# A DCN ranker on one core: ScalarE hands the copies out of PSUM to VectorE and fetches more embedding rows one by one

## The chip, the cores and the metric

One Trainium2 chip, of which the kernel uses one core. The metric is the device time of one launch in microseconds (us), the median of several runs; lower is better. In the traces PE is TensorE (PEld its weight loads), DVE is VectorE, ACT is ScalarE, POOL is GpSimd and SP is SyncE. A letter q behind an engine's name (ACTq, SPq) means its instruction queue: what the sequencer does without keeping the engine's lanes busy, such as issuing a DMA.

## What is computed

The reference, cut to what matters:

```python
def ref(ids, emb, cross_w, cross_b, w1, b1, w2, b2, w3, b3, out_w, out_b):
    x0 = emb[ids].reshape(2048, 26 * 64)      # 26 fields, rows of 64 floats, table of 125000 rows
    x = x0
    for i in range(3):
        s = x @ cross_w[i]
        x = x0 * s[:, None] + cross_b[i] + x
    h = relu(x0 @ w1 + b1)                    # 1664 -> 1024
    h = relu(h @ w2 + b2)                     # 1024 -> 512
    h = relu(h @ w3 + b3)                     # 512 -> 256
    return sigmoid(concatenate([x, h], axis=1) @ out_w + out_b)
```

All of it is float32. Every sample needs 26 rows of 256 bytes out of the embedding table.

## The kernel before

**Tiles.** The 2048 samples are 16 tiles of 128. For every tile the 26 embedding rows of each sample are gathered into `x_buf[t % 2]` (128 partitions by 1664 columns). A chunk is 128 of these columns, two fields; a tile has 13 chunks in four groups of 4, 3, 4 and 2 (`GROUPS`). For a group, VectorE patches rows whose index lies past the table (`make_whole`, L516; it also is the sign that the group is there), TensorE transposes its chunks into a PSUM bank (`transpose_x`, L729), and the transposed block is split into a high and a low part: ScalarE copies it out as `xT_hi` (`x_hi`, L400), VectorE subtracts that from the bank to give `xT_lo` (`x_lo`, L523). Each product of float32 matrices is then three matmuls, hi·hi, hi·lo and lo·hi (`three_passes`, L717). For `w1` a chunk is nine matmuls in three PSUM banks.

**A step.** In step t TensorE does layer 2 of tile t-1 and layer 1 of tile t, with transposes between the chunks; then it transposes `h1` of tile t (L771) and does layer 3 of tile t-1. The hidden layers are split as the inputs are: ScalarE makes `h1T_hi` (L406) and `h2T_hi` (L411) with a Relu, VectorE the low parts (L528). VectorE also adds the biases (L535, L544, L562). Step 0 also loads and splits the weights, and the last step has code of its own.

**Who fetches the rows.** GpSimd gathers one field of a tile with one indirect DMA (L347). Its order is field by field, held back by waits on `chunk_done` (`PACED`, `BEHIND`) and by `other_engines_turn`. A few fields are left out of it (`of_pool`) and are fetched row by row, 128 small DMAs for a field of a tile: SyncE takes field 24 in nine tiles (L295), ScalarE field 25 in seven tiles (L387), 400 fields being left for GpSimd. Both load the byte addresses into registers first (L292, L384) and write into small landing buffers, four of SyncE's and two of ScalarE's. When all 128 rows are there, ScalarE copies them into `x_buf` (`sp_place` L372, `act_place` L394). Group 3, the last of a tile, is the one whose `make_whole` waits for these copies.

**ScalarE's order.** It runs in program order: in a step it issues shares of 8, 12, 4, 16, 12 and 12 rows (64 in all), and between them come its six copies out of PSUM and the placing.

```python
            def step(t):
                fetch(ACT_SHARES[0])
                x_hi(t, 0)
                fetch(ACT_SHARES[1])
                h2_hi(t - 1)
                fetch(ACT_SHARES[2])
                x_hi(t, 1)
                fetch(ACT_SHARES[3])
                x_hi(t, 2)
                ...
```

The functions that the diff touches, with what calls them:

Of the kernel before, what the change touches and what calls it, by code (L numbers as in the profile page):

```python
# [5 lines left out]
def dcn_ranker_kernel(nc, r_ids, emb, cross_w, cross_b, w1, b1, w2, b2, w3, b3, out_w, out_b, out):  # L6
# [29 lines left out]
    def groups(t):  # L36
        return LAST_GROUPS if t == TILES - 1 else GROUPS
# [6 lines left out]
    LOW_BITS = 2 ** (H.bit_length() - 1) - 1  # L44


    SP_TILES = [2, 4, 6, 8, 9, 10, 12, 14, 15]
    SP_REGS = 32
    SP_FIELD = F - 2
    SP_BUFS = 4  # L50
    assert SP_FIELD // FPK in GROUPS[-1] and SP_FIELD // FPK in LAST_GROUPS[3]

    ACT_TILES = [3, 5, 7, 9, 11, 13, 15]
    ACT_FIELD = F - 1
    ACT_BUFS = 2
    ACT_SHARES = [8, 12, 4, 16, 12, 12]
    assert ACT_FIELD // FPK in GROUPS[-1] and all(
        sum(ACT_SHARES) * (t - 1) >= P * (j + 1) for j, t in enumerate(ACT_TILES)) and P % sum(ACT_SHARES) == 0  # L60


    ROW = E * 4
# [43 lines left out]
    with ctx:  # L107
# [44 lines left out]
        act_rows = [ids[:, (SP_BUFS + j) * E:(SP_BUFS + j + 1) * E].bitcast(F32) for j in range(ACT_BUFS)]  # L152
        sp_cols = ids[:, (SP_BUFS + ACT_BUFS) * E:(SP_BUFS + ACT_BUFS) * E + ONE_BY_ONE].bitcast(F32)
        at_bytes = sb("at_bytes", [ONE_BY_ONE, P], I32)
        at_row = {t: i for i, t in enumerate([t for t in SP_TILES if t % 2 == 0] + [t for t in SP_TILES if t % 2])}

        VR = (2 * CROSS + 1) * K1
        vec_rows = sb("vec_rows", [VR, P])
# [117 lines left out]
        @block.sync  # L276
        def _(sync):
            sync.dma_start(ids[:, :], r_ids.rearrange("(p t) f -> p (t f)", p=P)).then_inc(ids_loaded, 16)
            for n, (name, k, m) in enumerate(LOADS):
                src = {"w1": w1, "w2": w2, "w3": w3}[name][k * P:(k + m) * P, :].rearrange("(m p) c -> p m c", m=m)  # L280
                sync.dma_start(parts(n)[0], src).then_inc(weights_loaded[n], 16)

            sync.wait_ge(idx_ready, 3)
            for rows, vec in ((b1_rows, b1), (b2_rows, b2), (b3_rows, b3), (out_w_rows, out_w[D:D + N3, 0]), (out_b_rows, out_b)):
                sync.dma_start(rows[:, :], vec.rearrange("(o n) -> o n", o=1).broadcast_to([P, rows.shape[1]])).then_inc(rows_loaded, 16)
            sync.wait_ge(sp_idx_ready, 1)
            for i, t in enumerate(SP_TILES):
                if i >= SP_BUFS:
                    sync.wait_ge(sp_placed, i - SP_BUFS + 1)
                for p in range(0, P, SP_REGS):  # L290
                    regs = [sync.alloc_register(f"sp_row{i}_{p + j}") for j in range(SP_REGS)]
                    sync.load(regs, at_bytes[at_row[t]:at_row[t] + 1, p:p + SP_REGS])  # L292
                    for j, reg in enumerate(regs):
                        at = sync.snap(reg, donate=True, min_val=0, max_val=(2 * H - 1) * ROW)
                        sync.dma_start(sp_rows[i % SP_BUFS][p + j:p + j + 1, :].bitcast(U8),  # L295
                                       emb_bytes[:, bass.DynSlice(at, ROW)], bounds_check="skip_entire_dma").then_inc(sp_landed[i % SP_BUFS], 16)
            sync.wait_ge(result_ready, 2)
            sync.dma_start(out[:, 0].rearrange("(p t) -> p t", p=P), result[:, :]).then_inc(stored, 16)
            sync.wait_ge(stored, 16)
# [50 lines left out]
        def _(act):  # L350
# [13 lines left out]
            def split_hi(n):  # L364
                raw, hi, _ = parts(n)
                act.wait_ge(weights_loaded[n], 16)
                act.activation(hi, raw, ACT.Copy).then_inc(hi_split, 1)

            def sp_place(t):
                i = SP_TILES.index(t)  # L370
                act.wait_ge(sp_landed[i % SP_BUFS], 16 * P * (i // SP_BUFS + 1))
                act.activation(x_buf[t % 2][:, SP_FIELD * E:(SP_FIELD + 1) * E], sp_rows[i % SP_BUFS],  # L372
                               ACT.Copy).then_inc(sp_placed, 1)
# [2 lines left out]

            def fetch(share):

                j, p = fetched[0] // P, fetched[0] % P
                if p == 0 and j >= ACT_BUFS:  # L380
                    act.wait_ge(act_placed, j - ACT_BUFS + 1)
                row = len(SP_TILES) + j
                regs = [act.alloc_register(f"act_row{j}_{p + i}") for i in range(share)]
                act.load(regs, at_bytes[row:row + 1, p:p + share])  # L384
                for i, reg in enumerate(regs):
                    at = act.snap(reg, donate=True, min_val=0, max_val=(2 * H - 1) * ROW)
                    act.dma_start(act_rows[j % ACT_BUFS][p + i:p + i + 1, :].bitcast(U8),  # L387
                                  emb_bytes[:, bass.DynSlice(at, ROW)], bounds_check="skip_entire_dma").then_inc(act_landed[j % ACT_BUFS], 16)
                fetched[0] += share

            def act_place(t):
                j = ACT_TILES.index(t)
# [33 lines left out]
            def first_step():  # L426
                for g in range(NG):
                    for n in HI_AHEAD[g]:
                        split_hi(n)
                        if n == 0:  # L430
                            cross_hi()
                    x_hi(0, g)
                h1_hi(0)

            def step(t):
                fetch(ACT_SHARES[0])
                x_hi(t, 0)
                fetch(ACT_SHARES[1])
                h2_hi(t - 1)
                fetch(ACT_SHARES[2])  # L440
                x_hi(t, 1)
                fetch(ACT_SHARES[3])
                x_hi(t, 2)
                if t in SP_TILES:
                    sp_place(t)
                if t in ACT_TILES:
                    act_place(t)
                fetch(ACT_SHARES[4])
                x_hi(t, 3)
                fetch(ACT_SHARES[5])  # L450
                h1_hi(t)

            def last_step(t):
                x_hi(t, 0)
                h2_hi(t - 1)
                x_hi(t, 1)
                x_hi(t, 2)
                if t in SP_TILES:
                    sp_place(t)
                if t in ACT_TILES:  # L460
                    act_place(t)
                for g in range(3, len(LAST_GROUPS)):
                    x_hi(t, g)
                h1_hi_last(t)
                h2_hi_last(t)
# [20 lines left out]
        def _(dve):  # L486
# [16 lines left out]
            def make_whole(t, g):  # L503
# [10 lines left out]
                if t in ACT_TILES and ACT_FIELD in range(a, a + n):  # L514
# [2 lines left out]
                                    past[:, t * F + a:t * F + a + n].rearrange("p (f o) -> p f o", o=1).broadcast_to([P, n, E]),  # L517
                                    end_bank.rearrange("p (o e) -> p o e", o=1).broadcast_to([P, n, E])).then_inc(x_whole, 1)

            def x_lo(t, g):  # L520
                dve.wait_ge(xT_hi_ready, NG * t + g + 1)
                ks = groups(t)[g]
                dve.tensor_tensor(xT_lo[:, ks[0]:ks[-1] + 1, :].rearrange("p k b -> p (k b)"), x_bank[g % 2][:, 0:len(ks) * P],  # L523
                                  xT_hi[:, ks[0]:ks[-1] + 1, :].rearrange("p k b -> p (k b)").bitcast(F32),
                                  ALU.subtract).then_inc(xT_ready, 1)
# [40 lines left out]

            def h1_lo(t):
                for half in range(2):
                    dve.wait_ge(h1T_hi_ready, 2 * t + half + 1)
                    part = slice(half * HB, (half + 1) * HB)  # L570
                    relu_lo(h_bank[half], HB * P, h1T_hi[:, part, :].rearrange("p k b -> p (k b)"),
                            h1T_lo[:, part, :].rearrange("p k b -> p (k b)"), h1T_ready)
# [61 lines left out]
                dots_out(0)  # L634
                h1_lo(0)

            def begin(t):
                make_whole(t, 0)
                x_lo(t, 0)
                l2_out(t - 1)  # L640
                h2_lo(t - 1)
                make_whole(t, 1)
                x_lo(t, 1)

            def step(t):
                begin(t)
                for g in range(2, NG):
                    make_whole(t, g)
                    x_lo(t, g)
                l1_out(t)  # L650
                dots_out(t)
                h1_lo(t)
                l3_out(t - 1)

            def last_step(t):
                begin(t)
                l3_out(t - 1)
                for g in range(2, len(LAST_GROUPS)):
                    make_whole(t, g)
# [30 lines left out]
            link(dve.tensor_scalar(past[:, 0:QUICK], ids[:, 0:QUICK], float(H), None, ALU.is_ge))  # L690
            dve.wait_ge(idx_ready, 3)
            copied = 0
            for field, tiles in ((SP_FIELD, [t for t in SP_TILES if t % 2 == 0]), (SP_FIELD, [t for t in SP_TILES if t % 2]),
                                 (ACT_FIELD, ACT_TILES)):
                every = tiles[1] - tiles[0]
                assert tiles == list(range(tiles[0], tiles[-1] + 1, every))
                a, b = (t * F + field for t in (tiles[0], tiles[-1]))
                dve.scalar_tensor_tensor(out=sp_cols[:, copied:copied + len(tiles)], in0=past[:, a:b + 1:every * F], scalar=float(H),
                                         in1=idx[:, a:b + 1:every * F], op0=ALU.mult, op1=ALU.add).then_inc(sp_cols_ready, 1)
                copied += len(tiles)  # L700
# [11 lines left out]
        def _(pe):  # L712
# [195 lines left out]
            pe.transpose(h_bank[0][:, 0:VR], vec_rows[:, :], identity[0:VR, 0:VR]).then_inc(vecs_transposed, 1)  # L908
            pe.wait_ge(cross_ready, 1)

            pe.wait_ge(sp_cols_ready, 3)
            pe.transpose(x_bank[1][0:ONE_BY_ONE, 0:P], sp_cols, identity[:, :]).then_inc(sp_cols_transposed, 1)
            pe.wait_ge(sp_idx_ready, 1)
            pe.wait_ge(identity_r_set, 1)
# [30 lines left out]
```

## Time and profile before

| | |
|---|---|
| median of 3 runs | 529.95 us (529.79 to 530.59) |
| profiled execution: its own time | 530.56 us |
| profiled execution: span of its instructions | 528.8 us |
| busy: PE, DVE, ACT, POOL | 91%, 35%, 16%, 72% |
| rows fetched one by one: SyncE, ScalarE | 1152, 896 |
| indirect gathers of GpSimd | 400 |

The busy share of an engine does not count the time in which its queue issues DMAs. ACT's 16% therefore says nothing of how full its queue is; that is to be read from the rows of ACTq. The 1.76 us between the span and the execution's own time lie around the instructions.

### The profile page before, as it was taken

What the parts mean: (1) busy time and instruction counts of PE and PEld (TensorE: products, weight loads), DVE (VectorE), ACT (ScalarE), POOL (GpSimd) and SP (SyncE); (2) the same over time, 40 slices, a digit from 0 to 9 for tenths busy, and PEclk for the clock granted to TensorE, in tenths of its full rate; (3) what the DMA queues carried; (4) which work ended last, traced back from release to release, by engine and by line L of the source; (5) the groups of instructions that cost most, each with busy time, mean ns of one, the idle gap of its engine ahead of it and who ended that gap; (6) DMA issues with size and microseconds to landing.
All of it is one profiled execution on the core that took longest, in us unless ns stands there. A gap on an engine that the chain in (4) does not pass through costs nothing.

```text
span 528.8 us, 11324 instructions
## 1 busy us (share of the span) xinstructions
PE 480.8 (91%) x2912; PEld 442.2 (84%) x2912; DVE 186.4 (35%) x391; ACT 84.7 (16%) x159; POOL 379.6 (72%) x407
## 2 busy tenths in 40 slices
PE   2699899899999989899898989999899898999997
PEld 1399698898989889798887988888898888989996
DVE  5766414232142423224242321424232142423325
ACT  4642111111011111102011110101111010101111
POOL 5777776777777777777777777777777777777720
PEclk9999999999999999999999999999999999999999
DMA  7971111111111111111111111111111111111100
GB/s 234 387 263 29 28 29 27 28 29 27 29 29 29 28 28 30 29 29 29 27 29 26 30 27 30 26 30 29 26 30 25 30 27 28 27 28 28 28 10 2
DMA packets 19700, 24.90 MB, mean 47 GB/s; under 512 B 9305, under 2 KB 10292, under 8 KB 19636
## 3 DMA queue, kind: packets, MB, share of 16 engines
q0 software_dynamic: 12800, 13.13, 11.2%
q1 hardware_dynamic: 4770, 10.74, 5.7%
q10 hardware_dynamic: 2066, 0.31, 0.3%
q8 instruction: 23, 0.38, 0.3%
q14 instruction: 41, 0.34, 0.2%
HBM read 24.41 MB, written 0.01 MB: 46 GB/s over the span
## 4 chain that ended last, share of the span: by engine, by line
PE 55%; POOL 14%; issue 10%; ACTq 9%; DMA 5%; DVE 4%; ACT 3%; POOLq 0%; DVEq 0%
PE l_bank L717 41%; POOL x_raw L347 14%; ACTq L387 8%; DMA x_raw<-in_L_rec_emb,idx 4%; PE x_bank L717 4%; PE x_bank L729 4%; PE h_bank L771 3%; ACT xT_hi L400 2%; DVE x_raw L516 2%; ACTq L384 1%; PE l_bank L802 1%; DVE xT_lo L523 1%; PE h_bank L741 1%; DVE h2T_lo L528 1%; ACT h2T_hi L411 1%
## 5 line engine op out<-in xcount | busy, mean ns | idle before, releaser
L347 POOL DMA_INDIRECT x_raw<-in_L_rec_emb,idx x400 | 378.8, 947 | 125.5 <-issue 107.7
L717 PE MATMUL l_bank<-w_hi,xT_hi 128*128 128x342 f32 (+1 forms) x624 | 144.9, 333 | 3.5 <-DVE xT_lo L523 3.3
L717 PE MATMUL l_bank<-w_lo,xT_hi 128*128 128x342 f32 (+1 forms) x624 | 137.9, 321 | 0.0
L717 PE MATMUL l_bank<-w_hi,xT_lo 128*128 128x342 f32 (+1 forms) x624 | 137.7, 321 | 0.0
L717 PEld LDWEIGHTS l_bank<-w_hi,xT_hi 128*128 128x128 f32 x624 | 104.0, 191 | 7.9 <-DVE xT_lo L523 5.6
L717 PEld LDWEIGHTS l_bank<-w_lo,xT_hi 128*128 128x128 f32 x624 | 106.8, 191 | 0.0
L717 PEld LDWEIGHTS l_bank<-w_hi,xT_lo 128*128 128x128 f32 x624 | 106.3, 190 | 0.0
L523 DVE TENSOR_TENSOR xT_lo<-x_bank,xT_hi 128x512 fp32r<-128x512 f32 (+1 forms) x66 | 38.2, 578 | 158.5 <-ACT xT_hi L400 158.5
L400 ACT ACTIVATE xT_hi<-x_bank 128x512 fp32r<-128x512 f32 (+1 forms) x66 | 33.5, 507 | 270.3 <-PE x_bank L729 220.4
L729 PE MATMUL x_bank<-identity,x_raw 128*128 128x128 f32 x208 | 34.7, 279 | 27.0 <-DVE x_raw L516 27.0
L729 PEld LDWEIGHTS x_bank<-identity,x_raw 128*128 128x128 f32 x208 | 25.0, 142 | 36.7 <-issue 31.0
L516 DVE COPY_PREDICATED x_raw<-past,x_bank 128x512 f32<-128x512 int32 (+1 forms) x66 | 39.9, 605 | 42.7 <-DMA x_raw<-in_L_rec_emb,idx 42.7
L717 PE MATMUL l_bank<-w_hi,h1T_hi 128*128 128x512 f32 x120 | 48.7, 406 | 0.9 <-DVE h1T_lo L528 0.9
L717 PE MATMUL l_bank<-w_hi,h1T_lo 128*128 128x512 f32 x120 | 47.4, 395 | 0.0
L717 PE MATMUL l_bank<-w_lo,h1T_hi 128*128 128x512 f32 x120 | 47.2, 393 | 0.0
L535 DVE TENSOR_TENSOR h<-l_bank,b_rows 128x344 f32<-128x344 f32 (+2 forms) x48 | 23.2, 513 | 49.4 <-PE l_bank L717 49.4
L406 ACT ACTIVATE h1T_hi<-h_bank 128x512 fp32r<-128x512 f32 x30 | 17.6, 598 | 82.1 <-PE h_bank L771 82.1
L717 PEld LDWEIGHTS l_bank<-w_hi,h1T_lo 128*128 128x128 f32 x120 | 22.5, 188 | 5.3
L717 PEld LDWEIGHTS l_bank<-w_hi,h1T_hi 128*128 128x128 f32 x120 | 22.6, 188 | 5.0 <-DVE h1T_lo L528 1.1
L717 PEld LDWEIGHTS l_bank<-w_lo,h1T_hi 128*128 128x128 f32 x120 | 22.6, 189 | 4.1
L528 DVE SCALAR_TENSOR_TENSOR h2T_lo<-h_bank,h2T_hi 128x512 fp32r<-128x512 f32 (+1 forms) x16 | 10.8, 675 | 36.6 <-ACT h2T_hi L411 35.0
L528 DVE SCALAR_TENSOR_TENSOR h1T_lo<-h_bank,h1T_hi 128x512 fp32r<-128x512 f32 (+1 forms) x32 | 20.2, 670 | 9.8 <-ACT h1T_hi L406 9.7
(94 smaller groups left out, 296.5 us busy)
## 6 DMA issues: line engine op xcount, KB each, us to landing
ids<-in_L_rec_emb SPq DMA_DIRECT2D x1152, 0.2 KB
ids<-in_L_rec_emb ACTq DMA_DIRECT2D x896, 0.2 KB
w_raw<-in_L_rec_w SPq DMA_DIRECT2D x18, 512.0 KB, 15.0
x_raw<-in_L_rec_emb,idx POOLq DMA_INDIRECT x400, 2.4
b_rows<-in_L_rec_b SPq DMA_DIRECT2D x1, 512.0 KB
b_rows<-in_L_rec_b SPq DMA_DIRECT2D x1, 256.0 KB
ids<-in_r_ids SPq DMA_DIRECT2D x1, 208.0 KB, 2.7
b_rows<-in_L_rec_b SPq DMA_DIRECT2D x1, 128.0 KB
```

Source lines behind the costliest of these rows:

```text
L347: pool.indirect_dma_start(out=dst, out_offset=None, in_=emb, in_offset=rows).then_inc(landed, 16)
L384: act.load(regs, at_bytes[row:row + 1, p:p + share])
L387: act.dma_start(act_rows[j % ACT_BUFS][p + i:p + i + 1, :].bitcast(U8), emb_bytes[:, bass.DynSlice(at, ROW)], bounds_check="skip_entire_dm ...
L400: act.activation(xT_hi[:, ks[0]:ks[-1] + 1, :].rearrange("p k b -> p (k b)"), x_bank[g % 2][:, 0:len(ks) * P], ACT.Copy).then_inc(xT_hi_re ...
L406: act.activation(h1T_hi[:, half * HB:(half + 1) * HB, :].rearrange("p k b -> p (k b)"), h_bank[half][:, 0:HB * P], ACT.Relu).then_inc(h1T_ ...
L516: dve.copy_predicated(x_buf[t % 2][:, a * E:(a + n) * E].rearrange("p (f e) -> p f e", e=E), past[:, t * F + a:t * F + a + n].rearrange("p ...
L523: dve.tensor_tensor(xT_lo[:, ks[0]:ks[-1] + 1, :].rearrange("p k b -> p (k b)"), x_bank[g % 2][:, 0:len(ks) * P], xT_hi[:, ks[0]:ks[-1] + ...
L528: dve.scalar_tensor_tensor(out=lo, in0=bank[:, 0:cols], scalar=0.0, in1=hi.bitcast(F32), op0=ALU.max, op1=ALU.subtract).then_inc(done, 1)
L535: dve.tensor_tensor(h1[:, a:e], bank[:, 0:e - a], b1_rows[:, a:e], ALU.add).then_inc(h1_ready, 1)
L717: done = pe.matmul(bank[:, 0:b - a], x[:, k, :], w[:, k, a:b], start=(k == 0 and n == 0), stop=(k == last_k and n == 2))
L729: done = pe.transpose(x_bank[g % 2][:, i * P:(i + 1) * P], x_buf[t % 2][:, k * P:(k + 1) * P], identity[:, :])
L771: done = pe.transpose(bank[:, i * P:(i + 1) * P], h1[:, k * P:(k + 1) * P], identity[:, :])
```

## The change

ScalarE makes no copies out of PSUM in tiles 1 to 14. `x_hi`, `h1_hi` and `h2_hi` of these tiles become instructions of VectorE (`tensor_copy`, and `tensor_scalar` with a maximum), each right in front of the low part that belongs to it; `h2_hi` and `h2_lo` move behind group 1 of the inputs. Tiles 0 and 15 stay as they were. ScalarE's step is now: wait until group 0 of the tile is transposed, place the fetched fields of the tile, issue shares of 24, 28, 24 and 28 rows (104). The fields fetched one by one are 21 by SyncE, in all 13 tiles from 2 to 14, and 20 by ScalarE, in ten tiles; 393 fields are left for GpSimd. Fields 20 and 21 are chunk 10, the last of group 2. The five loads of bias rows move from SyncE to ScalarE's first step.

```diff
-    SP_TILES = [2, 4, 6, 8, 9, 10, 12, 14, 15]
+    SP_TILES = list(range(2, TILES - 1))
-    SP_FIELD = F - 2
+    SP_FIELD = GROUPS[2][-1] * FPK + 1
-    ACT_TILES = [3, 5, 7, 9, 11, 13, 15]
-    ACT_FIELD = F - 1
+    ACT_TILES = [3, 4, 5, 6, 8, 9, 10, 11, 13, 14]
+    ACT_FIELD = GROUPS[2][-1] * FPK
-    ACT_SHARES = [8, 12, 4, 16, 12, 12]
+    ACT_SHARES = [24, 28, 24, 28]
+    ONE_RUNS = [(SP_FIELD, range(2, TILES - 1)), (ACT_FIELD, range(3, 7)), (ACT_FIELD, range(8, 12)), (ACT_FIELD, range(13, 15))]
...
-            sync.wait_ge(idx_ready, 3)
-            for rows, vec in ((b1_rows, b1), (b2_rows, b2), (b3_rows, b3), (out_w_rows, out_w[D:D + N3, 0]), (out_b_rows, out_b)):
-                sync.dma_start(rows[:, :], vec.rearrange("(o n) -> o n", o=1).broadcast_to([P, rows.shape[1]])).then_inc(rows_loaded, 16)
...
+            def load_rows():
+                act.wait_ge(idx_ready, 3)
+                for rows, vec in ((b1_rows, b1), (b2_rows, b2), (b3_rows, b3), (out_w_rows, out_w[D:D + N3, 0]), (out_b_rows, out_b)):
+                    act.dma_start(rows[:, :], vec.rearrange("(o n) -> o n", o=1).broadcast_to([P, rows.shape[1]])).then_inc(rows_loaded, 16)
...
             def fetch(share):
+                while share > 0 and fetched[0] < P * len(ACT_TILES):
+                    j, p = fetched[0] // P, fetched[0] % P
+                    if p == 0 and j >= ACT_BUFS:
+                        act.wait_ge(act_placed, j - ACT_BUFS + 1)
+                    row, rows = AT_ROWS.index((ACT_FIELD, ACT_TILES[j])), min(share, P - p)
+                    regs = [act.alloc_register(f"act_row{j}_{p + i}") for i in range(rows)]
+                    act.load(regs, at_bytes[row:row + 1, p:p + rows])
+                    for i, reg in enumerate(regs):
+                        at = act.snap(reg, donate=True, min_val=0, max_val=(2 * H - 1) * ROW)
+                        act.dma_start(act_rows[j % ACT_BUFS][p + i:p + i + 1, :].bitcast(U8),
+                                      emb_bytes[:, bass.DynSlice(at, ROW)], bounds_check="skip_entire_dma").then_inc(act_landed[j % ACT_BUFS], 16)
+                    fetched[0] += rows
+                    share -= rows
...
+                    if g == 1:
+                        load_rows()
                     x_hi(0, g)
                 h1_hi(0)
 
             def step(t):
-                fetch(ACT_SHARES[0])
-                x_hi(t, 0)
-                fetch(ACT_SHARES[1])
-                h2_hi(t - 1)
-                fetch(ACT_SHARES[2])
-                x_hi(t, 1)
-                fetch(ACT_SHARES[3])
-                x_hi(t, 2)
+                if t in SP_TILES or t in ACT_TILES:
+                    act.wait_ge(x_transposed, NG * t + 1)
                 if t in SP_TILES:
                     sp_place(t)
                 if t in ACT_TILES:
                     act_place(t)
-                fetch(ACT_SHARES[4])
-                x_hi(t, 3)
-                fetch(ACT_SHARES[5])
-                h1_hi(t)
+                for share in ACT_SHARES:
+                    fetch(share)
...
+            def x_hi(t, g):
+                dve.wait_ge(x_transposed, NG * t + g + 1)
+                ks = groups(t)[g]
+                dve.tensor_copy(xT_hi[:, ks[0]:ks[-1] + 1, :].rearrange("p k b -> p (k b)"),
+                                x_bank[g % 2][:, 0:len(ks) * P]).then_inc(xT_hi_ready, 1)
+            def relu_hi(bank, cols, hi, done):
+                dve.tensor_scalar(hi, bank[:, 0:cols], 0.0, None, ALU.max).then_inc(done, 1)
...
             def h1_lo(t):
                 for half in range(2):
+                    if t > 0:
+                        h1_hi(t, half)
...
+            def step(t):
+                make_whole(t, 0)
+                x_hi(t, 0)
+                x_lo(t, 0)
+                l2_out(t - 1)
+                make_whole(t, 1)
+                x_hi(t, 1)
+                x_lo(t, 1)
+                h2_hi(t - 1)
+                h2_lo(t - 1)
+                for g in range(2, NG):
+                    make_whole(t, g)
+                    x_hi(t, g)
+                    x_lo(t, g)
+                l1_out(t)
+                dots_out(t)
+                h1_lo(t)
+                l3_out(t - 1)
```

## Rows read from the trace of the kernel before

**Rows 1.** The page: busy us of each engine, share of the span, instructions.

```profile
PE 480.8 (91%) x2912; PEld 442.2 (84%) x2912; DVE 186.4 (35%) x391; ACT 84.7 (16%) x159; POOL 379.6 (72%) x407
```

**Rows 2.** The page: the chain that ended last, by engine.

```profile
PE 55%; POOL 14%; issue 10%; ACTq 9%; DMA 5%; DVE 4%; ACT 3%; POOLq 0%; DVEq 0%
```

**Rows 3.** The view of waits: engine, line, whom it waited for, us in total.

```profile
DVE x_raw L516 <- DMA x_raw<-in_L_rec_emb,idx: 42.7, 19, 3.8
```

**Rows 4.** The chain in order of time, tiles 13 and 14: start, us, what.

```profile
457.92 2.77 PE l_bank L717 x12
...
475.68 0.61 ACT xT_hi L400
...
477.06 4.52 PE l_bank L717 x27
```

**Rows 5.** Timeline of ScalarE: start, us, queue or engine, instruction, count [idle before].

```profile
54.05 1.12 ACT L406 ACTIVATE h1T_hi<-h_bank 128x512 fp32r<-128x512 f32 x2 [6.01 <-PE h_bank L771]
...
95.10 0.60 ACT L411 ACTIVATE h2T_hi<-h_bank 128x512 fp32r<-128x512 f32 x1 [4.63 <-PE h_bank L813]
95.78 1.44 ACTq L387 DMA_DIRECT2D ids<-in_L_rec_emb  x4
97.61 0.49 ACT L400 ACTIVATE xT_hi<-x_bank 128x384 fp32r<-128x384 f32 x1 [1.92 <-PE x_bank L729]
98.91 5.38 ACTq L387 DMA_DIRECT2D ids<-in_L_rec_emb  x16
...
104.83 0.25 ACT L372 ACTIVATE x_raw<-ids 128x64 f32<-128x64 f32 x1
...
109.75 0.38 ACT L400 ACTIVATE xT_hi<-x_bank 128x256 fp32r<-128x256 f32 x1 [4.67 <-PE x_bank L729]
110.89 4.10 ACTq L387 DMA_DIRECT2D ids<-in_L_rec_emb  x12
```

**Rows 6.** Single lines: durations in ns, min/median/max, first and last start.

```profile
L387 ACTq DMA_DIRECT2D ids<-in_L_rec_emb x896: 234/235/532, 55.4 to 486.7; - x180
L384 ACTq TENSOR_LOAD <-at_bytes x84: 486/966/1203, 54.6 to 481.8; - x84
L295 SPq DMA_DIRECT2D ids<-in_L_rec_emb x1152: 42/73/318, 32.1 to 356.4; - x192
```

**Rows 7.** VectorE's timeline: `make_whole` of group 2, tiles 2, 3, 13; a subtraction.

```profile
99.34 0.73 DVE L516 COPY_PREDICATED x_raw<-past,x_bank 128x512 f32<-128x512 int32 x1 [0.65 <-DMA x_raw<-in_L_rec_emb,idx]
...
130.92 0.74 DVE L516 COPY_PREDICATED x_raw<-past,x_bank 128x512 f32<-128x512 int32 x1 [1.65 <-DMA x_raw<-in_L_rec_emb,idx]
...
442.25 0.72 DVE L516 COPY_PREDICATED x_raw<-past,x_bank 128x512 f32<-128x512 int32 x1 [3.75 <-DMA x_raw<-in_L_rec_emb,idx]
444.74 0.69 DVE L523 TENSOR_TENSOR xT_lo<-x_bank,xT_hi 128x512 fp32r<-128x512 f32 x1 [1.76 <-ACT xT_hi L400]
```

**Rows 8.** Stretches: busy us (count) of each engine, granted clock, DMA share, GB/s.

```profile
60.00:442.00 382.00, 356.57 (x2196) 331.25 (x2194) 118.67 (x233) 49.00 (x98) 288.20 (x305) 1.00 0.13 28
442.00:517.00 75.00, 72.12 (x454) 67.98 (x454) 24.67 (x54) 10.30 (x25) 48.33 (x52) 1.00 0.11 24
```

**Rows 9.** Timeline of SyncE's queue, and its longest wait.

```profile
24.29 4.13 SPq L285 DMA_DIRECT2D b_rows<-in_L_rec_b  x3
...
32.06 324.43 SPq L295 DMA_DIRECT2D ids<-in_L_rec_emb  x1152
...
SPq L292 <- ACT x_raw L372: 27.9, 1, 27.9
```

**Rows 10.** Timeline of ScalarE in step 0, where the bias loads would go.

```profile
33.61 0.49 ACT L400 ACTIVATE xT_hi<-x_bank 128x384 fp32r<-128x384 f32 x1 [6.14 <-PE x_bank L729]
```

**Rows 11.** Timeline of TensorE in step 0, before and after its clock rose.

```profile
25.96 1.06 PE L717 MATMUL l_bank<-w_lo,xT_hi 128*128 128x344 f32 x3
...
31.66 0.64 PE L717 MATMUL l_bank<-w_lo,xT_hi 128*128 128x344 f32 x3
```

**Rows 12.** GpSimd's gathers as one group: busy us, mean ns, idle before.

```profile
L347 POOL DMA_INDIRECT x_raw<-in_L_rec_emb,idx x400 | 378.8, 947 | 125.5 <-issue 107.7
```

More of the change, by code:

```diff
@@ L44, in dcn_ranker_kernel @@
     LOW_BITS = 2 ** (H.bit_length() - 1) - 1
-    SP_TILES = [2, 4, 6, 8, 9, 10, 12, 14, 15]
+    SP_TILES = list(range(2, TILES - 1))
     SP_REGS = 32
-    SP_FIELD = F - 2
+    SP_FIELD = GROUPS[2][-1] * FPK + 1
     SP_BUFS = 4
-    assert SP_FIELD // FPK in GROUPS[-1] and SP_FIELD // FPK in LAST_GROUPS[3]
-    ACT_TILES = [3, 5, 7, 9, 11, 13, 15]
-    ACT_FIELD = F - 1
+    ACT_TILES = [3, 4, 5, 6, 8, 9, 10, 11, 13, 14]
+    ACT_FIELD = GROUPS[2][-1] * FPK
     ACT_BUFS = 2
-    ACT_SHARES = [8, 12, 4, 16, 12, 12]
-    assert ACT_FIELD // FPK in GROUPS[-1] and all(
-        sum(ACT_SHARES) * (t - 1) >= P * (j + 1) for j, t in enumerate(ACT_TILES)) and P % sum(ACT_SHARES) == 0
+    ACT_SHARES = [24, 28, 24, 28]
+    assert all(sum(ACT_SHARES) * (t - 1) >= P * (j + 1) for j, t in enumerate(ACT_TILES))
+    ONE_RUNS = [(SP_FIELD, range(2, TILES - 1)), (ACT_FIELD, range(3, 7)), (ACT_FIELD, range(8, 12)), (ACT_FIELD, range(13, 15))]
+    AT_ROWS = [(f, t) for f, tiles in ONE_RUNS for t in tiles]
+    assert sorted(AT_ROWS) == sorted([(SP_FIELD, t) for t in SP_TILES] + [(ACT_FIELD, t) for t in ACT_TILES])
     ROW = E * 4
@@ L154, in dcn_ranker_kernel @@
         at_bytes = sb("at_bytes", [ONE_BY_ONE, P], I32)
-        at_row = {t: i for i, t in enumerate([t for t in SP_TILES if t % 2 == 0] + [t for t in SP_TILES if t % 2])}
         VR = (2 * CROSS + 1) * K1
@@ L291, in _ @@
                     regs = [sync.alloc_register(f"sp_row{i}_{p + j}") for j in range(SP_REGS)]
-                    sync.load(regs, at_bytes[at_row[t]:at_row[t] + 1, p:p + SP_REGS])
+                    row = AT_ROWS.index((SP_FIELD, t))
+                    sync.load(regs, at_bytes[row:row + 1, p:p + SP_REGS])
                     for j, reg in enumerate(regs):
@@ L377, in fetch @@
             def fetch(share):
[L379 to L389, printed above, removed]
+                while share > 0 and fetched[0] < P * len(ACT_TILES):
[11 more added lines that the diff above has]
+                    share -= rows
             def act_place(t):
@@ L447, in step @@
                     act_place(t)
-                fetch(ACT_SHARES[4])
-                x_hi(t, 3)
-                fetch(ACT_SHARES[5])
-                h1_hi(t)
+                for share in ACT_SHARES:
+                    fetch(share)
             def last_step(t):
+                assert t not in SP_TILES and t not in ACT_TILES
                 x_hi(t, 0)
                 h2_hi(t - 1)
[L456 to L462, printed above, removed]
+                for g in range(1, len(LAST_GROUPS)):
                     x_hi(t, g)
@@ L518, in make_whole, with h1_hi, h2_hi @@
                                     end_bank.rearrange("p (o e) -> p o e", o=1).broadcast_to([P, n, E])).then_inc(x_whole, 1)
+            def x_hi(t, g):
[5 more added lines that the diff above has]
+                dve.tensor_scalar(hi, bank[:, 0:cols], 0.0, None, ALU.max).then_inc(done, 1)
+            def h1_hi(t, half):
+                dve.wait_ge(h1_transposed, 2 * t + half + 1)
+                relu_hi(h_bank[half], HB * P, h1T_hi[:, half * HB:(half + 1) * HB, :].rearrange("p k b -> p (k b)"), h1T_hi_ready)
+            def h2_hi(t):
+                dve.wait_ge(h2_transposed, t + 1)
+                relu_hi(h_bank[0], K3 * P, h2T_hi[:, :, :].rearrange("p k b -> p (k b)"), h2T_hi_ready)
             def x_lo(t, g):
@@ L635, in first_step, with last_step @@
                 h1_lo(0)
-            def begin(t):
+            def step(t):
[16 more added lines that the diff above has]
+                l3_out(t - 1)
+            def last_step(t):
                 make_whole(t, 0)
@@ L643, in begin @@
                 x_lo(t, 1)
[L645 to L656, printed above, removed]
                 l3_out(t - 1)
@@ L692, in _ @@
             copied = 0
[L693 to L697, printed above, removed]
+            for field, tiles in ONE_RUNS:
+                a, b, every = tiles[0] * F + field, tiles[-1] * F + field, tiles.step
                 dve.scalar_tensor_tensor(out=sp_cols[:, copied:copied + len(tiles)], in0=past[:, a:b + 1:every * F], scalar=float(H),
@@ L909, in _ @@
             pe.wait_ge(cross_ready, 1)
-            pe.wait_ge(sp_cols_ready, 3)
+            pe.wait_ge(sp_cols_ready, len(ONE_RUNS))
             pe.transpose(x_bank[1][0:ONE_BY_ONE, 0:P], sp_cols, identity[:, :]).then_inc(sp_cols_transposed, 1)
```

## The prediction

> **What bounds the kernel now.** I read the page first. TensorE is busy for 91% of the span, ScalarE for 16% and VectorE for 35% [rows 1], so by busy shares the change moves work from one idle engine to another. The chain that ended last says otherwise: GpSimd has 14% of it, and ScalarE's queue, whose issues count as idle time, has 9% [rows 2]. The waits show GpSimd's part: `make_whole`, without which TensorE gets no group, waited 42.7 us for gathers [rows 3]. A gather costs 0.947 us and, in 107.7 us of issue over some 360 gaps, 0.3 us more, 1.25 us; 400 of them fill 500 us [rows 12]. ScalarE's part is seen in step 14: the copy of group 2 starts at 475.68, when the 16 rows issued ahead of it are out, and TensorE starts on it at 477.06 [rows 4]. The steps are 31.1 us long (group 2 of tile 3 at 130.92, of tile 13 at 442.25 [rows 7]), and TensorE is busy for 356.6 of 382 us of them [rows 8], 29 us a step. So the kernel is bound by TensorE, by GpSimd with 31.2 us for 25 gathers, and by ScalarE's queue as a third that is almost full. The last is what this change turns on, so I read that queue next.
>
> **What a row costs ScalarE.** In [rows 5] a share can be timed whole, its register load included, from the start of the copy in front of it to the end of its last issue. Four rows: 95.10 to 97.22, 2.12 us. Sixteen rows: 97.61 to 104.29, 6.68 us. That is 4.56 us for 12 more rows, 0.38 us a row, and 0.60 us a share. Shares of twelve agree, with 5.24 us (109.75 to 114.99) against 5.16. The single lines say the same: an issue takes 234 ns at the least and 235 in the median over 896 rows, and the register load grows from 486 to 1203 ns with the share. SyncE's issue of the same DMA takes 73 ns [rows 6]. ScalarE's price does not hang on SyncE: SyncE's issues end at 356.5 [rows 9], ScalarE's go on to 486.7, and least and median are one nanosecond apart.
>
> **The change, part by part.**
>
> *Rows of ScalarE.* I take 0.38 us a row and 0.70 a share (0.60, and 0.10 for the step to the next and for a late issue now and then). Four shares of 104 rows are 39.5 + 2.8 = 42.3 us. Nothing stands between them, and nothing is taken off them: the copies that leave took the lanes 0.60 us each, while the time here is the queue's. So ScalarE's step is 42.3 us where the kernel's is 31. This is the term that decides.
>
> *When ScalarE falls behind.* It starts fetching when the second copy of [rows 5]'s first line has started, 54.05 + 1.12 - 0.60 = 54.6. Step 1 ends at 96.9, and the placing of tile 2 just precedes 99.34, when `make_whole` of group 2 ran before [rows 7]. Step 2 ends at 139.2; tile 3's was at 130.92, and it now waits 8 to 9 us. From then on every step waits. Twelve steps issue 1248 rows; eight field boundaries fall inside a share and split it, which makes 56 shares. 1248 x 0.38 + 56 x 0.70 = 513.4 us, and about 1 us for the placing. Step 13 starts at 54.6 + 514.4 = 569.0, and two placings of 0.25 us [rows 5] put group 2 of tile 13 at 569.5. It was at 442.25 [rows 7]: 127.2 us later. Step 13 fetches only the last 32 rows, some 13.5 us, so ScalarE is on time for tile 14, and tile 15 needs none.
>
> *What is queued behind it.* ScalarE waits for group 0 of a tile and places only at the start of its step, so a placement never overtakes the shares in front of it. `make_whole` of group 2 waits for it; behind that on VectorE are the split of groups 2 and 3 and the biases; TensorE has one chunk of group 1 left before it needs the transposes of group 2, and stops; GpSimd stops too, since its field 4 of the next tile waits for that transpose. After the placing TensorE needs some 18 us to the first transposes of the next tile (442.25 to 457.92 + 2.77 = 460.69 [rows 4, 7]), well inside 42.
>
> *VectorE's new copies.* Seven a step. The trace has none; the nearest row is the subtraction from the same bank, 0.69 us for 512 columns [rows 7]. With the smaller groups 7 x 0.6 = 4.2 us come on top of 118.7 / 382 x 31 = 9.6 busy [rows 8]. On the way from the transposes to the low part a VectorE copy replaces ScalarE's 0.60: nothing, or 0.2 us either way. The Relus of `h1` in line on VectorE end 1.2 us later, under layer 3 and the first half of layer 2, of which the latter alone takes 2.77 [rows 4]. All of it is hidden by the wait for the placing; uncovered in steps 13 and 14 it is at most 1 us.
>
> *Seven gathers fewer.* 7 x 1.25 = 8.75 us of GpSimd. GpSimd waits in every step now, so worth nothing. Only the end could use it: TensorE idles 2.9 us between 442 and 517 [rows 8], half of it in front of group 2 of tile 13; I take 1.4 off.
>
> *SyncE.* 1152 rows in 324.4 - 27.9 us are 0.257 each, 33 us a field [rows 9]. Starting right behind the weights at 24.3, with a first load of 2 us, it has tile 14 at 26 + 13 x 33 = 455, always ahead of ScalarE's placing. Nothing.
>
> *The bias loads.* On SyncE the three large ones of the five took 4.13 us [rows 9], so some 5.5 us in all; ScalarE is idle for 6.14 us in front of 33.61, where they go [rows 10]. Nothing, and 3 us if ScalarE issues them half as fast again.
>
> *TensorE's clock.* In each stall it idles about 42.3 - 31.1 = 11 us. The granted clock reads 1.00 in every stretch [rows 8], but the durations tell the two levels apart: in step 0, after an idle start, three matmuls took 1.06 us at 25.96 and 0.64 at 31.66 [rows 11], 1.2 GHz and then 2.4. In the steps bound by ScalarE slow matmuls are covered. After the last stall they are not: nine threes at 0.42 more, 3.8 us, with 0 and 8 as the ends. The Trainium skill ("TensorE: Matmul & The Clock Gate", Part 1) says that a TensorE left idle goes back to the lower clock and has to earn the higher one by work; by that rule this term is above nothing, without it it is nothing, and step 0 agrees with the rule.
>
> *Sum.* Span 528.8 + 127.2 - 1.4 + 3.8 = 658.4; around it 1.76 us, so 660.2 against that execution's own 530.56. The median of the runs lies 0.6 below the profiled one. I predict **659.5 us**, 24% slower.
>
> *Bounds of the main term.* If a row costs what the line-up of parts gives, (4.10 - 0.235) / 11 = 0.35 and 0.06 of load, it is 0.41: 37 us more. If the long shares are cheaper, with the share's own 0.6 us gone, 34 us less. Both ends rest on one step each; the whole shares lie between, and I keep half of either way.
>
> **Rivals.** (1) *ScalarE's queue becomes cheap without copies in it* (faster). If its issue fell to SyncE's 73 ns, a row would cost 0.22 and a step 26 us, under the kernel's 31. Then GpSimd's 8.75 us come off: 521.8. It decides at (31 - 2.8) / 104 = 0.27 us a row. For it: one queue does it. Against it: the least of 896 issues is 234 ns, and shares of 16 hold issues that are 5 us behind the last copy [rows 5]. Chance 0.05. (2) *The register load does not grow with the share*: 1.0 us each. It grew by (1203 - 486) / 12 = 60 ns a row so far, so 1248 x 0.06 come off and 56 x 0.7 are put on: 36 less, 624. Against it: the loads of [rows 6]. 0.04. (3) *TensorE stays at its lower clock after every stall.* Its step would be 29 us and 39 threes at 0.42 more and 12 of layers 2 and 3 at about 0.5 more, 51, which is 9 over 42.3. Ten steps of that, and an end of 87 us at the lower clock with 60 more, make about 810. Against it: in step 0 it rose between 25.96 and 31.66, while at work [rows 11]. 0.03. (4) *VectorE's new copies hold GpSimd up* for as long as they run. 4.2 us a step on GpSimd's 24 x 1.25 = 30 make 34, 3 us over 31; with ScalarE as cheap as in (1) that gives 530.6 + 13 x 3 = 570. Beside a step of 42.3 it changes nothing. Against it: with VectorE's present work beside them the gathers take 947 ns in the mean [rows 12]. 0.02. The Trainium skill ("SBUF — State Buffer", Who interferes with whom) has plain copies of VectorE, in a two-port mode, shut GpSimd out for the whole instruction. The copies here read PSUM, and no row of this trace shows one of their size.
>
> **Chances.** The forecast, bound by ScalarE's issue at about the price of before, has 0.86, and its own range is 636 to 684: half of the two bounds of a row (18 us), with the clock's 4 us either way and up to 3 for the bias loads. The rivals have 0.05, 0.04, 0.03 and 0.02. The range of 636 to 684 holds all of the forecast's cases but some 5 in 100, so 8 in 10, and reaches to none of the rivals. A measurement of this kernel tells 0.2% from no change. Faster by more has 0.05, within it 0.02 (rival 1 with its gain eaten by later copies), slower 0.93.
>
> **What would show it.** ACTq L387 issues back to back at about 235 ns from 55 to nearly 580, 1280 of them. The starts of L372 and L394 42 to 43 us apart from tile 3 to 13. `make_whole` of group 2 waiting some 10 us for ScalarE in each of these tiles, and TensorE idle there; TensorE's busy share near 75%. No wait of DVE for gathers to speak of. After each stall matmuls at the longer duration. The prediction is wrong if the least duration of an ACTq issue falls below 0.2 us, or if ScalarE's step ends before the next group 0.

## The result, and the profile after

The changed kernel takes 515.57 us (median of 4 runs, 515.41 to 515.84) against 529.87 for the kernel before in the same session: a ratio of 0.973, with a 95% interval of 0.9713 to 0.9747. The forecast was 659.5 us. The change was to make the kernel 24% slower, and it made it 2.7% faster.

The page of the changed kernel: the span, the busy shares, the chain by engine, and GpSimd's gathers.

```profile
span 513.8 us, 13128 instructions
...
PE 478.8 (93%) x2912; PEld 444.7 (87%) x2912; DVE 247.9 (48%) x490; ACT 33.5 (7%) x68; POOL 372.1 (72%) x400
...
PE 61%; POOL 18%; issue 11%; DMA 6%; DVE 3%; ACT 0%; POOLq 0%; DVEq 0%
...
L345 POOL DMA_INDIRECT x_raw<-in_L_rec_emb,idx x393 | 371.2, 945 | 122.2 <-issue 107.6
```

Against [rows 1, 2, 12]: VectorE went from 35% to 48%, ScalarE's queue has left the chain, and what is left of it is TensorE and GpSimd.

The single lines that answer to [rows 6] (L391 is ScalarE's issue, L388 its register load, L293 SyncE's issue; min/median/max in ns), and two steps of ScalarE's timeline:

```profile
L391 ACTq DMA_DIRECT2D ids<-in_L_rec_emb x1280: 88/90/517, 55.0 to 430.7; - x183
...
L388 ACTq TENSOR_LOAD <-at_bytes x58: 481/1702/2048, 53.2 to 428.5; - x58
...
L293 SPq DMA_DIRECT2D ids<-in_L_rec_emb x1664: 73/73/323, 26.7 to 454.2; - x185
```

```profile
146.50 0.26 ACT L375 ACTIVATE x_raw<-ids 128x64 f32<-128x64 f32 x1 [29.70 <-PE x_bank L745]
146.66 0.24 ACT L399 ACTIVATE x_raw<-ids 128x64 f32<-128x64 f32 x1
148.32 27.74 ACTq L391 DMA_DIRECT2D ids<-in_L_rec_emb  x104
176.16 0.26 ACT L375 ACTIVATE x_raw<-ids 128x64 f32<-128x64 f32 x1 [29.26 <-PE x_bank L745]
176.32 0.24 ACT L399 ACTIVATE x_raw<-ids 128x64 f32<-128x64 f32 x1
178.00 28.87 ACTq L391 DMA_DIRECT2D ids<-in_L_rec_emb  x104
206.97 0.26 ACT L375 ACTIVATE x_raw<-ids 128x64 f32<-128x64 f32 x1 [30.41 <-issue]
```

This is the surprise. ScalarE issues a row in 90 ns in the median where it took 235 before, while a register load costs what it did for the same number of rows, and SyncE's line did not move. So 104 rows with their loads take 28.3 to 30.3 us from step 2 on (from the end of the placing to the end of the last issue), not 42.3. The steps are 30.2 us long in the mean. The placings start 29.7 and 30.8 us apart. The brackets name TensorE for the first two and ScalarE's own issues for the third, but it was the queue each time: group 0 of tile 4 had been transposed at 145.74, the last issue ended at 146.40, and the placing began at 146.50, 0.10 us behind it, as in nine steps of the first eleven. The queue is full, then, yet it holds nothing up: that placing comes 10 us before `make_whole` of group 2, at 156.86, which needs it.

VectorE's timeline around group 2 of tile 5 (at 192.90 before), and `make_whole` of group 3:

```profile
186.75 0.72 DVE L510 COPY_PREDICATED x_raw<-past,x_bank 128x512 f32<-128x512 int32 x1 [2.10 <-DMA x_raw<-in_L_rec_emb,idx]
188.29 0.69 DVE L517 CAST xT_hi<-x_bank 128x512 fp32r<-128x512 f32 x1 [0.81 <-PE x_bank L745]
189.01 0.69 DVE L534 TENSOR_TENSOR xT_lo<-x_bank,xT_hi 128x512 fp32r<-128x512 f32 x1
191.78 0.45 DVE L510 COPY_PREDICATED x_raw<-past,x_bank 128x256 f32<-128x256 int32 x1 [2.07 <-DMA x_raw<-in_L_rec_emb,idx]
```

In these tiles `make_whole` waits for GpSimd's gathers, not for a placing; the new copy takes 0.69 us for 512 columns, as the nearest row did.

### The profile page after: what moved, and what is told of

Its sections match the earlier page's. It is cut to its first block, busy times and chain, and to the rows that moved or that the text cites. A ratio compares the mean times of both kernels' runs of the same rounds, so it can differ in the third digit from the quotient of the medians.

```text
span 513.8 us, 13128 instructions
## 1 busy us (share of the span) xinstructions
PE 478.8 (93%) x2912; PEld 444.7 (87%) x2912; DVE 247.9 (48%) x490; ACT 33.5 (7%) x68; POOL 372.1 (72%) x400
## 4 chain that ended last, share of the span: by engine, by line
PE 61%; POOL 18%; issue 11%; DMA 6%; DVE 3%; ACT 0%; POOLq 0%; DVEq 0%
PE l_bank L733 50%; POOL x_raw L345 18%; DMA x_raw<-in_L_rec_emb,idx 6%; PE x_bank L745 4%; PE x_bank L733 2%; PE h_bank L787 2%; DVE x_raw L510 2%; PE l_bank L818 1%; PE h_bank L757 1%; DMA ids<-in_r_ids 1%; PE h_bank L829 0%; PE l_bank L757 0%; DVE xT_lo L534 0%; PE h_bank L733 0%; DVE xT_hi L517 0%
## 5 line engine op out<-in xcount | busy, mean ns | idle before, releaser
L345 POOL DMA_INDIRECT x_raw<-in_L_rec_emb,idx x393 | 371.2, 945 | 122.2 <-issue 107.6
L517 DVE CAST xT_hi<-x_bank 128x512 fp32r<-128x512 f32 (+2 forms) x56 | 33.1, 592 | 94.2 <-PE x_bank L745 94.2
L745 PEld LDWEIGHTS x_bank<-identity,x_raw 128*128 128x128 f32 x208 | 26.1, 143 | 24.2 <-issue 18.7
L375 ACT ACTIVATE x_raw<-ids 128x64 f32<-128x64 f32 x13 | 3.3, 257 | 396.1 <-PE x_bank L745 210.4
L539 DVE SCALAR_TENSOR_TENSOR h1T_lo<-h_bank,h1T_hi 128x512 fp32r<-128x512 f32 (+1 forms) x32 | 21.5, 675 | 1.8 <-ACT h1T_hi L411 0.7
L787 PE MATMUL h_bank<-identity,h 128*128 128x128 f32 x124 | 20.5, 286 | 0.8 <-DVE h L546 0.8
```

Source lines behind the costliest of these rows:

```text
L345: pool.indirect_dma_start(out=dst, out_offset=None, in_=emb, in_offset=rows).then_inc(landed, 16)
L517: dve.tensor_copy(xT_hi[:, ks[0]:ks[-1] + 1, :].rearrange("p k b -> p (k b)"), x_bank[g % 2][:, 0:len(ks) * P]).then_inc(xT_hi_ready, 1)
L539: dve.scalar_tensor_tensor(out=lo, in0=bank[:, 0:cols], scalar=0.0, in1=hi.bitcast(F32), op0=ALU.max, op1=ALU.subtract).then_inc(done, 1)
L745: done = pe.transpose(x_bank[g % 2][:, i * P:(i + 1) * P], x_buf[t % 2][:, k * P:(k + 1) * P], identity[:, :])
L787: done = pe.transpose(bank[:, i * P:(i + 1) * P], h1[:, k * P:(k + 1) * P], identity[:, :])
```

## The experiments

Four theories were tried on the price of an issue: what stands between the shares (A), the size of a share (B), the row that is fetched (C), the new program as such (D).

**e1, shares of 8.**

```diff
-    ACT_SHARES = [24, 28, 24, 28]
+    ACT_SHARES = [8] * 13
```

> The changed kernel with ScalarE's 104 rows in 13 shares of 8 in place of 24, 28, 24, 28; still no copy between them. Theory A (what stands between the shares sets the price: copies out of PSUM made every issue slow): the median issue stays at 90 ns, the step has nine more loads of some 0.5 us of fixed cost and slow first issues, so some 6 us more, and the time is within 2 us of the changed kernel's 515.6 or a few us over it. Theory B (short shares are what made an issue cost 235 ns): the median goes back to 235 ns, ScalarE's step to over 42 us, and the time to some 660 us.

534.2 us, ratio 1.007 (1.0055 to 1.0086) to the kernel before. The median issue stayed at 90 ns: B is out. The time is far over the "few us" of the expectation:

```profile
86.51 0.26 ACT L375 ACTIVATE x_raw<-ids 128x64 f32<-128x64 f32 x1 [32.26 <-PE x_bank L745]
87.35 33.18 ACTq L391 DMA_DIRECT2D ids<-in_L_rec_emb  x104
120.63 0.26 ACT L375 ACTIVATE x_raw<-ids 128x64 f32<-128x64 f32 x1 [33.86 <-issue]
```

Nine more loads make ScalarE's step 34.1 us here (86.51 to 120.63) and 32.6 in the mean of ten, over the kernel's 30. The 10 us that the placings have in hand are used up by tile 5; from tile 6 to tile 13 `make_whole` of group 2 starts within 0.7 us of a placing, and the kernel's steps are as long as ScalarE's: some 18 us lost. What the forecast described is real, it only begins at another price: ScalarE's queue becomes the bound when its step stays over 30 us long enough to use up its lead.

**e2, the copies alone.** The changed kernel with the fields, tiles and shares of before.

```diff
-    SP_TILES = list(range(2, TILES - 1))
+    SP_TILES = [2, 4, 6, 8, 9, 10, 12, 14, 15]
-    SP_FIELD = GROUPS[2][-1] * FPK + 1
+    SP_FIELD = F - 2
-    ACT_TILES = [3, 4, 5, 6, 8, 9, 10, 11, 13, 14]
-    ACT_FIELD = GROUPS[2][-1] * FPK
+    ACT_TILES = [3, 5, 7, 9, 11, 13, 15]
+    ACT_FIELD = F - 1
-    ACT_SHARES = [24, 28, 24, 28]
+    ACT_SHARES = [8, 12, 4, 16, 12, 12]
```

> Only the copies move to VectorE (and the bias loads to ScalarE): fields, tiles and shares of 8, 12, 4, 16, 12 and 12 rows are those of the kernel before, 400 gathers. Theory A: the issues fall to about 90 ns, as no copy stands between the shares; B: they stay at 235. Under both ScalarE's queue holds nothing up, so the time shows what the copies alone bring: GpSimd keeps 400 gathers, 8.75 us more than in the changed kernel, so 522 to 525 us if it is the bound, and 516 if the seven gathers were worth nothing.

529.1 us, ratio 0.9969 (0.9957 to 0.9981). The issues stayed at 235 ns with no copy between them:

```profile
L391 ACTq DMA_DIRECT2D ids<-in_L_rec_emb x896: 234/235/529, 53.9 to 487.8; - x180
```

A is out too: taking the copies away does not make the issues cheap. The time missed both of the expected values (522 to 525, and 516); moving the copies brings 0.3% by itself. ScalarE's queue cost the kernel before less than its 9% of the chain suggests. The likely reason is that GpSimd was ready to take its place: the chain of e2 has 38% POOL, against 14% before.

**e4, a tiny instruction of ScalarE in front of each share.**

```diff
                 for share in ACT_SHARES:
+                    act.activation(tiny[:, c:c + 1], ones[:, 0:1], ACT.Copy)
                     fetch(share)
```

> The changed kernel with one tiny instruction of ScalarE (one column, SBUF to SBUF, no wait) in front of each of the four shares. Theory A in its wide form (any lane instruction between the shares makes the issues slow): 235 ns again and some 650 us. In its narrow form (only copies out of PSUM, or with waits, do): 90 ns but for the first few of each share, and within 1 us of 515.6.

516.1 us, median issue 90 ns: no effect.

**e5, before with its 64 rows in one place.**

> The kernel before with its six shares issued in one place, behind the copy of group 2; all its copies stay on ScalarE. Theory A: a run of 64 issues without a copy in between falls to 90 ns after the first few, although the copies are still in the program. Theory B: 235 ns throughout, as the shares are short. The copy of group 3 comes late behind 64 rows, by some 5 us a step at 90 ns and 15 at 235, so the time is 560 to 600 us under A and over 650 under B.

829.0 us in one run. No place among the 64 is under 234 ns in the median, so a long run does not make an issue cheap either. The time went far past what was expected, which had counted the issues alone (64 x 0.235 = 15 us); with the time between them and the register loads the 64 rows take 27.7 us. The copy of group 3 is 28 us late in each step, and TensorE, idle so long, runs at a granted clock of 0.80 in the stretch below (columns as in [rows 8]).

```profile
122.00:174.00 52.00, 30.68 (x182) 28.69 (x181) 9.74 (x19) 4.00 (x8) 23.88 (x26) 0.80 0.10 18
```

What e2 and e5 have in common with the kernel before, and e1 and e4 with the changed one, is the field. The reference draws the ids field by field. Fields 0 to 24 are drawn up to just under 1,000,000, for a table of 125,000 rows; the last one is `randint(..., 42, 124982)`. So every row of field 25 lies in the table. Of any other field about an eighth does, and the rest go past it. The row DMAs carry `bounds_check="skip_entire_dma"`, and `make_whole` patches those rows later in any case. The old `ACT_FIELD` is 25, the new one 20. That gave theory C.

**e6, the changed kernel with field 25.**

```diff
-    ACT_FIELD = GROUPS[2][-1] * FPK
+    ACT_FIELD = F - 1
```

> The changed kernel with one constant changed: ScalarE fetches field 25, as in the kernel before, in place of field 20. Theory C (an issue's price hangs on the row: field 25 is drawn below 125000, so all its rows lie in the table and are fetched at 235 ns; of any other field only an eighth does, and the rest is skipped by the bounds check at 90): the median issue goes back to 235 ns, ScalarE's step to 42 us, and the time to the 660 us of the prediction, or more if TensorE's clock falls in the stalls. Theory D (the new program, its loads or its order made the issues cheap): 90 ns and 515.6 us.

666.0 us, ratio 1.2557 (1.2538 to 1.2576). Issue, steps, and `make_whole` of group 2 in tile 3:

```profile
L391 ACTq DMA_DIRECT2D ids<-in_L_rec_emb x1280: 234/235/502, 55.9 to 589.6; - x183
```

```profile
183.75 0.26 ACT L375 ACTIVATE x_raw<-ids 128x64 f32<-128x64 f32 x1 [43.01 <-issue]
183.92 0.24 ACT L399 ACTIVATE x_raw<-ids 128x64 f32<-128x64 f32 x1
185.57 41.82 ACTq L391 DMA_DIRECT2D ids<-in_L_rec_emb  x104
227.49 0.26 ACT L375 ACTIVATE x_raw<-ids 128x64 f32<-128x64 f32 x1 [43.34 <-issue]
```

```profile
140.70 0.72 DVE L510 COPY_PREDICATED x_raw<-past,x_bank 128x512 f32<-128x512 int32 x1 [15.24 <-ACT x_raw L375]
```

One constant turns 515.6 us into 666.0. The traffic of ScalarE's queue shows why; the kernels are the changed one and then e6 (packets, MB, share):

```profile
q10 hardware_dynamic: 1334, 1.17, 0.7%
```

```profile
q10 hardware_dynamic: 3554, 1.46, 0.8%
```

0.29 MB more are some 1130 rows of 256 bytes, give or take 40. 1280 were issued in both; if all of field 25 landed, some 150 of field 20 did, about an eighth.

The changed kernel's own trace has the two prices side by side. Of ScalarE's 1280 issues 1110 take 88 to 108 ns and 170 take 227 to 517 (238 in the median). Five in a row, one of them dear:

```profile
L391 ACTq DMA_DIRECT2D ids<-in_L_rec_emb x5: 90/90/238, 152.6 to 153.4; - x5
```

Set beside the ids that the reference draws (row p of tile t is sample 16p + t), the 170 are the rows that lie in the table, every one, and the 1110 those that don't. C stands, and nothing about the program is needed to explain the price.

**e7, the kernel before with the fields of SyncE and ScalarE swapped.**

```diff
-    SP_FIELD = F - 2
+    SP_FIELD = F - 1
-    ACT_FIELD = F - 1
+    ACT_FIELD = F - 2
```

> The kernel before with the fields swapped: SyncE fetches 25, ScalarE 24; tiles, shares, copies, gathers stay. Theory C: the median issue of ScalarE falls from 235 to 90 ns and that of SyncE rises from 73 to about 235, in an otherwise unchanged program. D: both stay. By C ScalarE's shares are short and hold no copy up any more, SyncE needs 51 us a field and is still in time, so the time falls by what ScalarE's queue cost the kernel before: 1 to 5 us.

529.76 us, ratio 0.9986 (0.9977 to 0.9995): 0.7 us, at the edge of what can be told from nothing and less than the 1 to 5 expected. The two issue lines changed places (L387 ScalarE, L295 SyncE):

```profile
L387 ACTq DMA_DIRECT2D ids<-in_L_rec_emb x896: 90/90/552, 55.2 to 484.8; - x180
...
L295 SPq DMA_DIRECT2D ids<-in_L_rec_emb x1152: 227/228/328, 32.9 to 488.8; - x192
```

So the price belongs to the field, on either engine and in either program. Cheap issues on ScalarE, bought with dear ones on SyncE, bring next to nothing.

**e3 and e3b, the rows without the copies.** All that concerns the fetching is as in the changed kernel, and ScalarE keeps its copies, between shares of 14, 20, 8, 24, 18, 20 (e3) or 12, 20, 8, 24, 20, 20 rows (e3b).

> All that concerns the rows, and not the copies: fields 20 and 21, 13 and 10 tiles, 104 rows of ScalarE a step (in shares of 14, 20, 8, 24, 18, 20 between its copies), 393 gathers, bias loads on ScalarE; ScalarE keeps the copies out of PSUM. By C ScalarE's queue needs some 28 us of a step of 30 and gets its copies out late. If the rows are the whole gain: 515 to 517 us. If VectorE's copies are needed for it, as late copies hold TensorE up by 0.5 to 1 us a step: 520 to 530.

> As e3, the rows' part of the change without the copies' part, but with shares of 12, 20, 8, 24, 20 and 20 rows, so that each register load starts at a multiple of four rows (16 bytes); in e3 the loads that didn't took 0.15 us more for each register (20 registers in 4.5 us, against 1.4). If that was e3's loss, all loads here take 0.25 + 0.06 us a register, and the time falls from 662 to under 530. If the lost time is that of the copies, which stand behind shares of 20 and 24 rows on a queue that is full, each copy is still up to 6 us late and the time stays over 540 us.

e3 took 662.5 us, ratio 1.249 (1.2473 to 1.2507), with its issues at 90 ns, far from both expected values. Its register loads were long: 227 us in all, against 96 in e3b. One load of 20 registers in each, e3 and then e3b:

```profile
L388 ACTq TENSOR_LOAD <-at_bytes x1: 4626/4626/4626, 265.6 to 265.6; - x1
```

```profile
L388 ACTq TENSOR_LOAD <-at_bytes x1: 1467/1467/1467, 285.2 to 285.2; - x1
```

With aligned shares e3b took 542.5 us, ratio 1.022 (1.0206 to 1.0234): still slower than the kernel before. The expectation's "under 530" missed and its other branch came true, as this stretch of e3b shows:

```profile
263.62 4.63 ACTq L391 DMA_DIRECT2D ids<-in_L_rec_emb  x24
268.30 0.60 ACT L405 ACTIVATE xT_hi<-x_bank 128x512 fp32r<-128x512 f32 x1 [6.29 <-issue]
269.87 4.51 ACTq L391 DMA_DIRECT2D ids<-in_L_rec_emb  x20
274.43 0.39 ACT L405 ACTIVATE xT_hi<-x_bank 128x256 fp32r<-128x256 f32 x1 [5.53 <-issue]
```

Each copy starts when the share ahead of it is out. Together: copies alone 0.3% faster, rows alone 2.2% slower, both 2.7% faster. The copies had to leave not for their own time, but so that 104 rows could stand on that queue; other ways to place the shares between the copies were not tried.

**e9, fields 24 and 23 in place of 21 and 20; e10, seven gathers back.** e10 has `ACT_TILES = [5, 9, 13]` with 32 rows a step, and 400 gathers.

> The changed kernel with fields 24 (SyncE) and 23 (ScalarE), of group 3, in place of 21 and 20, of group 2; both fields have an eighth of their rows in the table. If only the number of gathers counts, 515.6 us. If it counts that the fields are the last of group 2, where GpSimd's gathers ended last in front of TensorE, then the time is 2 to 5 us longer, as in the gap that e2 leaves: 13.5 us to the changed kernel, of which seven gathers explain 8.75.

> The changed kernel with ScalarE fetching field 20 in three tiles (5, 9, 13) in place of ten, 32 rows a step: 400 gathers, as in the kernel before. The seven gathers are the one difference to the changed kernel in GpSimd's work. If GpSimd is the bound that the rows relieve, 7 x 1.25 = 8.75 us more than 515.6: 524.4. If other things made the gain (the fields' place in group 2, the copies), it stays near 516.

e9: 519.33 us, ratio 0.9796 (0.9782 to 0.9809). e10: 524.71 us, ratio 0.9893 (0.9878 to 0.9908), where 524.4 was expected. The kernel before took 529.87 to 530.61 us beside the different runs, so differences between runs are taken here by their ratios to it, times 529.87; each is good to about 1 us. Seven gathers are then 8.6 us between e10 and the changed kernel, 1.2 us each, the whole price of a gather. (e10 also takes ScalarE's queue from 104 rows a step to 32; as its placings come 7 us or more early in both, that should cost or bring nothing, but it was not tried alone.) The place in group 2 is 3.5 us. And with 400 gathers in both, the fields and tiles of the change (e10) beat those of before (e2) by 4.0 us.

**e11, eleven tiles.** ScalarE fetches 40 rows in step 0 and 108 a step from step 10 on; 392 gathers.

> An attempt at a better version: ScalarE fetches 8, 16 and 16 rows in the idle time of its first step and 108 in place of 104 from step 10 on, so that field 20 is its in eleven tiles: 392 gathers. If a gather is worth 1.25 us: 514.4. If ScalarE's queue, at 28.5 us of a step of 30, gets full: 516 or more.

514.95 us, ratio 0.9707 (0.9694 to 0.9721), the best median of all. Its interval overlaps that of the changed kernel's 0.973, so that it beats it isn't settled. ScalarE's queue is full there: its placings in steps 11 to 13 begin 0.1 us after its own last issue, 31.2 and 30.9 us apart, and still 7 us or more before `make_whole` of group 2.

## Why the prediction was wrong

**The step that failed** is the first of the sum, "I take 0.38 us a row", with "nothing is taken off them". The 235 ns were measured on field 25 and carried over to field 20. The diff's `ACT_FIELD` line stood in the change, and I read it as a place in the order of groups only. Measured: a step of four shares takes 29.7 us in the changed kernel and 43.0 in e6 (the brackets of the first placing shown of each). The difference over 104 rows is 0.13 us a row; the mean issue is 119 ns in the changed kernel and 246 in e6, 0.127 us apart.

**Rival 1 happened, for a reason that I had not seen.** I gave it 0.05, since "the least of 896 issues is 234 ns". That minimum was the hint: ScalarE's issues had no cheap one among 896, and SyncE's had two prices (73 in the median, 318 at most, [rows 6]). In the trace of the kernel before, 1015 of SyncE's 1152 issues take 42 to 102 ns and 137 take 227 to 318, about an eighth. The same instruction on two queues, with one and with two prices, asks what differs in the data, and the reference had the answer; the trace of the kernel before, read issue by issue, was enough to settle it. Its condition was right: it put the turning point at 0.27 us a row, and (29.7 - 2.8) / 104 = 0.26 was measured. e1, with ScalarE's step 2.4 us over the changed kernel's in the mean, lost some 18 us. Its price, 521.8, was 6 too high: 8.75 us for the gathers was right (8.6 in e10), and the place in group 2 (3.5, e9) and the copies (1.6, e2) were missing from it.

**The mechanism behind the main case was right and is e6**: 666.0 us against 659.5. ScalarE's step was 43.6 us (group 2 of tile 3 at 140.70, of tile 13 at 576.76) and not the 42.9 that the forecast has in the mean (514.4 us in twelve steps). The waits stood where they were said to, VectorE for the placing (15.24 us in tile 3) and TensorE behind it.

**TensorE's clock** in e6: after each stall the threes take 1.06 us and then 0.62 to 0.64 again, the two levels of [rows 11], with these two of e6 2.5 us apart:

```profile
143.31 1.06 PE L733 MATMUL l_bank<-w_lo,xT_hi 128*128 128x344 f32 x3
...
145.81 0.62 PE L733 MATMUL l_bank<-w_lo,xT_hi 128*128 128x344 f32 x3
```

After the last stall, of 13.13 us, five threes ran slow and not nine, so 3.8 us was about twice too much. Rival 3 (it stays low) is out for stalls of 13 to 14 us. The Trainium skill ("TensorE: Matmul & The Clock Gate", Part 1) says that an idle TensorE falls back to the lower clock and gets the higher one again by work. This trace agrees, with the 1.06 us after an idle time of 14.38 us and the 0.62 behind it. In the changed kernel TensorE waits at most 2.6 us for `make_whole` and the granted clock is 0.99 in the mean, and the term is next to nothing.

**Other terms.** VectorE's copies were sized right (0.69 us) and do not hold GpSimd up. The 99 gathers that ran while VectorE made a high part take 944 ns in the mean and the other 294 take 945, against 947 before, so rival 4's mechanism does not show here. The bias loads stand in ScalarE's idle time, as forecast: they are out at 29 us, and its copy of group 1 waits for TensorE until 32.27. That "GpSimd waits in every step now, so worth nothing" fell with the first step; seven gathers fewer are the largest single gain.

**Where the 14.3 us came from**, as far as the runs separate them: copies off ScalarE 1.6 (before to e2), fields and tiles of the rows 4.0 (e2 to e10), seven gathers 8.6 (e10 to the changed kernel), each to about 1 us. They add up to 14.3 only in this order: with the copies left on ScalarE the rows cost time (e3b). e2 and e10 differ in group, tiles and shares together, and the 3.5 of e9 suggests that the group is most of it.

## What to carry to other kernels

A duration read from a trace holds for the data it was measured on: before it is carried to other rows, fields or indices, look at its spread, duration by duration and not only at the median, and at how the inputs are drawn. An engine that issues many small DMAs in program order delays whatever stands behind them on its queue; move that work away before the queue is filled, and work out at which price per DMA the queue becomes the bound. When several resources are nearly full, single edits understate a change or even change its sign, as rows and copies did here.

## What was not expected of the hardware

- A row DMA that the bounds check skips occupies the issuing queue for 90 ns on ScalarE and 73 on SyncE; one that is carried out takes 235 and 228 where all are (e6, e7), and 238 in the median on both where most of its neighbours are skipped (the changed kernel).
- A load of registers from SBUF costs about 0.25 us and 0.06 us for each register if it starts at a multiple of 16 bytes. Where a load's first row wasn't such a multiple, it took some 0.15 us more for each register: 4.63 us for 20 registers in e3, 1.47 in e3b. The shares' sizes differ between the two as well, but e3 alone tells them apart: of its loads of 20 registers ten start at such a multiple and take 1.3 to 1.5 us, and ten don't and take 4.4 to 4.6. All of the latter start 8 bytes past one; other offsets were not tried.
